# A convolution and scan kernel on one core: image pair 0 scans 131 steps ahead of pair 1

## The chip, the core and the metric

The kernel runs on one core of a Trainium2 chip. The core has a matrix engine (TensorE, PE in the rows; its weight loads are shown as PEld), a vector engine (VectorE, DVE), an activation engine (ScalarE, ACT), a general engine (GpSimd, POOL) and a sequencer for transfers (SyncE, SP). Each takes its own instructions in order and waits on semaphores for the others. The metric is the time of one execution on the device in microseconds (us), lower is better. The medians are of 3 runs. The profile is of one more execution, with the hardware's records switched on.

## What is computed

Four images of 48 channels and 128 x 128 pixels go through four layers, each added to its input after a group norm over the whole image (16 groups). All of it is in float32.

```python
x = x + L0(gn(x))   # channel attention: 1x1 conv, 3x3 depthwise, q k^T over pixels, softmax, v, 1x1
x = x + L1(gn(x))   # four scans
x = x + L2(gn(x))   # four scans with other weights
x = x + L3(gn(x))   # per pixel MLP: W1, gelu twice, layer norm, 3x3 and 1x1 conv of 8 channels, gate, W2

def step(w, b):                       # one step of a scan
    def f(carry, inp):                # carry: one line of 128 pixels, 48 channels
        nxt = inp + conv1d(carry, w, b)   # 5 taps along the line
        return nxt, nxt
```

The four scans of a layer go down the rows, back up, along the columns, and back. Each has 127 steps, and each step needs the line that the step before it made. The four images are independent until the end; only the group norm ties the pixels of one image together, and it has to see all of them.

## The kernel before, in words

**Layout.** An image's pixels lie two to a partition group: the 112 used partitions hold the channels of even pixels (LO) and odd pixels (HI). Images are stored by pairs: pair 0 is images 0 and 1, pair 1 is images 2 and 3. A line of one pair is 128 elements in each partition, and a scan step works on one pair.

**The attention (to 970.6 us).** For each image PE makes queries, keys and their gram product (`query_keys`, L834 to L849, 32 "pairs" of products per image, "qk" below) and then the output convolution (`output_conv`, L888, 16 groups of six products, "cv"). ACT stages the normalised input for both (`stage`, L625). The softmax of an image runs on DVE, ACT and PE in slots between the products of the next image. The order is qk0, qk1, cv0, qk2, cv1, qk3, cv2, cv3.

**The scans.** For layer and scan, for each of the 127 steps, both pairs take one step (both take part in one turn of the loop, here called a **beat**). A step of a pair is this chain: six matrix instructions on PE (three float32 products, each recorded twice: L927, L928, L930) add into a PSUM bank that already holds input plus bias; ACT copies the bank over the line in `image` (L718), and this copy releases the pair's next step. DVE has put input plus bias into the other bank of the pair meanwhile (`preload`, L1213, line 1213). In the second and fourth scan DVE also exchanges odd and even pixels of the finished lines for the next direction (`swap_part`, L1223, three copies of 256 elements for both pairs together, in three of every four slots). Lines are contiguous in scans one and two and strided in three and four.

**Between the layers (1676.5 to 1781.4 us).** The input of the layer comes back from DRAM in chunks of 2048 elements (`bring`, L399), DVE adds two of each four (L1233) and GpSimd the other two (L530), DVE takes the statistics (L1051), the sum is saved (L404), and ACT (L699) and DVE (L1254) normalise. PE waits.

**After the scans (2472.6 to 2648.3 us).** DVE (three of four parts) and GpSimd (one) add the residual and write 16 chunks in natural order (`natural`, recorded at L323, which both engines call), the chunks go to DRAM (L750) and come back as tokens, pixel major (L440). DVE takes statistics of all four images and `affine` (L1325) normalises image 0. Then the MLP runs image by image to the end.

**GpSimd elsewhere.** Early in the first scan it clears buffers (L498) and builds the banded weights of the 3x3 convolution with 120 small instructions (L510, L513, L517).

What sets the order is the program text: there is no planner. Each engine's list is written so that both pairs are in the same scan at the same step.

## Time and profile before

| | us |
|---|---|
| median of 3 runs (lowest to highest) | 2888.86 (2888.66 to 2891.61) |
| the profiled execution, its own time | 2902.14 |
| its span, first to last instruction | 2900.0 |
| PE busy | 2491.4 (86%) |
| DVE busy | 1597.3 (55%) |
| ACT busy | 1087.6 (38%) |
| POOL busy | 271.9 (9%) |
| mean granted clock of PE | 0.937 of 2.4 GHz |

The span in 40 slices (72.5 us each) shows PE at nine tenths or more nearly all the way, with a hole between the two scan layers and another behind the second. A busy PE is not a PE at its peak: the ends of matrix instructions are modelled. The granted clock is a share of 2.4 GHz and has two levels here, 1.0 and 0.5. The scan stretches hold 1016 beats in 1382 us, so a beat is the unit of what follows.

### The profile page before, as it was taken

To read this page: it belongs to the slowest core of one execution; us is meant where nothing else is said; L and a number is where in the kernel's file an instruction comes from. 1 tells how busy PE (TensorE), PEld (TensorE's weight loads), DVE (VectorE), ACT (ScalarE), POOL (GpSimd) and SP (SyncE) were. 2 spreads that over 40 slices of the span, in tenths; PEclk is the share of its full clock that TensorE was granted. 3 is DMA by queue.
4 is the path that set the end of the run, shared out by engine and by line. 5 is a ranking of instruction groups with operands and counts; after the bars stand their busy time and mean duration, and the time that the engine had idled before them with its cause. 6 is when DMAs were issued, how large, how long until landed. Compare 5 with 4: busy or idle time off the path is not lost.

```text
span 2900.0 us, 47470 instructions
## 1 busy us (share of the span) xinstructions
PE 2491.4 (86%) x18076; PEld 2178.8 (75%) x18076; DVE 1597.3 (55%) x3797; ACT 1087.6 (38%) x2617; POOL 271.9 (9%) x288
## 2 busy tenths in 40 slices
PE   1999999999999899999999914999999999104986
PEld 1999949949943599999999914999999999002443
DVE  2323223223322455885568875558855688775655
ACT  3533343343357344444444413444444444001221
POOL 1000000000000360000000041000000000335420
PEclk9999999999999999999999956999999999556998
DMA  8840000003001400000000076000000000474423
GB/s 147 143 78 2 1 1 1 1 0 88 1 0 44 88 1 1 2 2 1 1 2 1 2 201 147 1 1 2 2 1 1 1 1 2 130 235 170 117 87 87
DMA packets 51672, 130.17 MB, mean 45 GB/s; under 512 B 9120, under 2 KB 34048, under 8 KB 44896
## 3 DMA queue, kind: packets, MB, share of 16 engines
q1 hardware_dynamic: 48352, 113.92, 16.4%
q10 hardware_dynamic: 2976, 13.34, 1.5%
q8 instruction: 138, 2.26, 0.3%
q14 instruction: 78, 0.64, 0.1%
q0 software_dynamic: 128, 0.01, 0.0%
HBM read 76.91 MB, written 50.33 MB: 44 GB/s over the span
## 4 chain that ended last, share of the span: by engine, by line
PE 84%; DMA 6%; DVE 6%; issue 2%; ACT 1%; POOL 1%; SPq 0%; DVEq 0%; ACTq 0%; POOLq 0%
PE bank L927 17%; PE bank L928 15%; PE bank L930 15%; PE bank L834 13%; PE bank L888 11%; PE bank L849 3%; PE bank L839 3%; DMA flat_rows<-work 2%; DVE work L323 2%; DMA work<-saved 2%; PE bank L972 2%; PE bank L1030 1%; DMA work<-in_x 1%; DMA saved<-image 1%; PE bank L963 1%
## 5 line engine op out<-in xcount | busy, mean ns | idle before, releaser
L1213 DVE TENSOR_SCALAR bank<-image,scan_bias 112x128 f32<-112x128 f32 x2032 | 711.7, 360 | 354.8 <-ACT image L718 333.1
L718 ACT COPY image<-bank 112x128 f32<-112x128 f32 x2032 | 588.4, 290 | 795.1 <-PE bank L930 764.5
L927 PE MATMUL bank<-image,scan_wt 112*112 112x128 f32 x4064 | 816.9, 282 | 31.6 <-ACT image L699 16.8
L928 PE MATMUL bank<-image,scan_wt 112*112 112x126 f32 x4064 | 771.3, 271 | 0.0
L930 PE MATMUL bank<-image,scan_wt 112*112 112x126 f32 x4064 | 769.6, 270 | 0.0
L927 PEld LDWEIGHTS bank<-image,scan_wt 112*112 112x112 f32 x4064 | 557.2, 175 | 41.9 <-ACT image L699 27.2
L928 PEld LDWEIGHTS bank<-image,scan_wt 112*112 112x112 f32 x4064 | 581.8, 176 | 0.0
L930 PEld LDWEIGHTS bank<-image,scan_wt 112*112 112x112 f32 x4064 | 578.8, 176 | 0.0
L625 ACT ACTIVATE work<-image,gn_shift,gn_scale 48x567 f32<-48x567 f32 (+5 forms) x384 | 332.5, 898 | 348.9 <-PE bank L839 219.4
L834 PE MATMUL bank<-work 112*128 112x192 f32 x2304 | 424.4, 333 | 10.0 <-issue 10.0
L834 PEld LDWEIGHTS bank<-work 112*128 112x128 f32 x2304 | 375.8, 193 | 11.7 <-issue 11.2
L888 PE MATMUL bank<-work 112*112 112x512 f32 x768 | 333.0, 595 | 3.0 <-DVE work L1141 3.0
L888 PEld LDWEIGHTS bank<-work 112*112 112x112 f32 x768 | 135.8, 178 | 194.0 <-issue 190.8
L1109 DVE COPY work<-bank 128x384 f32<-128x384 f32 x128 | 71.4, 558 | 360.4 <-PE bank L839 276.6
L1051 DVE BATCH_NORM_STATS2 stats<-image 112x6 f32<-112x512 f32 (+2 forms) x240 | 152.9, 683 | 61.1 <-ACT image L597 45.1
L1162 DVE TENSOR_TENSOR image<-image,bank 112x512 f32<-112x512 f32 (+1 forms) x64 | 44.1, 690 | 238.3 <-PE bank L888 147.0
L809 PE MATMUL bank<-mean_var,group_flat 128*128 128x4 f32 x2 | 0.6, 366 | 169.7 <-DVE mean_var L1058 169.7
L323 POOL TENSOR_TENSOR work<-image,work 48x1024 f32<-48x1024 f32 x16 | 56.2, 3513 | 788.8 <-DVE image L1223 715.4
L809 PEld LDWEIGHTS bank<-mean_var,group_flat 128*128 128x128 f32 x2 | 0.5, 313 | 169.8 <-DVE mean_var L1058 169.8
L809 PE MATMUL bank<-mean_var,group_half 112*112 112x2 f32 (+2 forms) x12 | 2.5, 276 | 137.2 <-DVE mean_var L1058 137.2
L323 DVE TENSOR_TENSOR work<-image,work 48x1024 f32<-48x1024 f32 x48 | 98.6, 2053 | 35.4 <-DMA flat_rows<-work 33.4
L1223 DVE COPY work<-image 48x256 f32<-48x256 f32 x256 | 80.9, 316 | 66.5 <-ACT image L718 58.5
(137 smaller groups left out, 1639.0 us busy)
## 6 DMA issues: line engine op xcount, KB each, us to landing
work<-saved SPq DMA_DIRECT2D x64, 384.0 KB, 8.8
saved<-image SPq DMA_DIRECT2D x10, 1536.0 KB, 21.6
flat_rows<-work ACTq DMA_DIRECT2D x32, 384.0 KB, 7.3
image<-flat_rows SPq DMA_DIRECT2D x4, 3072.0 KB, 13.9
out<-image SPq DMA_DIRECT2D x8, 1536.0 KB, 8.1
saved<-image SPq DMA_DIRECT2D x12, 768.0 KB, 9.9
band<-in_x SPq DMA_DIRECT2D x16, 384.0 KB, 6.0
work<-in_x SPq DMA_DIRECT2D x16, 384.0 KB, 6.2
```

The costliest lines, as they stand in the source:

```text
L323: return eng.tensor_tensor(o[:, :, :, :, half], i0.rearrange("p g s k j -> p (g s) k j"), i1, ALU.add)
L625: last = nc.scalar.activation(dst.rearrange("p (k j) -> p k j", j=J2)[:, :, d[0]:d[1]], src, ACT.Identity, bias=gn_shift[part, b:b + 1], s ...
L718: nc.scalar.copy(line(g, along_w, at), state_bank(g, done)).then_inc(s_state[g], 1)
L834: last = mm(dst, (blk_z, blk_n)[buf][n % 2][:, o:o + 2 * J2], qk_w[buf][:, dy].rearrange("p a b -> p (a b)"), start=(t == 0), stop=(packed ...
L839: last = mm(dst[:, side * QK:(side + 1) * QK], blk_2[n % 2][:, side, sub, o:o + 2 * J2], qk_w2[:, side, :], start=False, stop=(side == 1))
L849: last = mm(bank_gram[0:QK, 0:QK], v, v, start=(i == 0 and c == 0), stop=(i == PAIRS - 1 and c == 3))
L888: last = mm(bank_out[sub][0:P, :], out_w[buf][:, dy, :], (blk_z, blk_n)[buf][n % 2][:, o:o + BLK * J2], start=(t == 0), stop=(t == len(pro ...
L927: mm(dst, wt[:, 1], src, start=False, stop=False, skip_group_check=True)
L928: mm(dst[:, 1:J2, :], wt[:, 0], src[:, 0:J2 - 1, :], start=False, stop=False, skip_group_check=True)
L930: mm(dst[:, 0:J2 - 1, :], wt[:, 2], src[:, 1:J2, :], start=False, stop=True, skip_group_check=True).then_inc(s_prod[g], 1)
L1051: return v.bn_stats(stat6[0:parts, b, ds(c * 6, 6)], src)
L1213: v.tensor_scalar(state_bank(g, done), line(g, along_w, src), scan_bias[:, 3 * layer + kind:3 * layer + kind + 1], None, ALU.add).then_inc ...
```

## The change

The change lets pair 0 run 131 steps ahead of pair 1 (`LEAD`). One function, `moment`, says for a pair and a beat in which layer, scan and step it is; 1204 beats (`BEATS`) take the place of 1016.

- **Beats 0 to 118** hold steps of pair 0 alone, one after each half of a qk3 pair (64), 7 around the softmax of image 3, and one after every second product of cv3 (48). cv2 therefore moves ahead of qk3. Pair 0 uses PSUM banks 5 and 6, pair 1 banks 2 and 3.
- **Beats 119 to 130** are pair 0 alone, with the group norm of pair 1 (`arrive`).
- **From beat 131** both pairs step in most beats. Each pair has two idle beats between its second and third scan, and a pause of 53 (`GAP`) between the layers. In that pause DVE adds two chunks in pieces of 512 elements and takes 32 statistics, one instruction per beat (`turn`), GpSimd adds the other six chunks in pieces of 512 and normalises half of the lines, and DVE and ACT normalise the rest. While one pair pauses, the other steps alone (beats 510 to 562 and 641 to 693).
- **Beats 1073 to 1203**: pair 1 alone. Pair 0 is converted: DVE does `natural` in 64 pieces of 256 elements, one per beat, GpSimd does two of four parts in pieces of 512, tokens are loaded, and 24 statistics and a norm follow.
- **Behind the last beat** the eight chunks of pair 1 are converted as before, by DVE (three parts) and GpSimd (one). `affine(0)` waits for the last conversion alone. The statistics of pair 1 (24) lie inside the MLP of image 0, its norm and `affine(2)` behind it.
- The exchange copies are per pair, 128 elements each, twice as many; in the fourth scan of the second layer there are none.
- GpSimd normalises all of pair 0 before its first scan and half of pair 1 (`normalise`); the buffers' clearing and the banded weights come after that. Loops of the MLP are unrolled. Buffers move; `xn` and several tiles of the MLP now lie in `work`.

The core of the diff ("..." marks what is left out):

```diff
+V_CHUNKS = (0, PER)
+P_CHUNKS = tuple(c for c in range(2 * PER) if c not in V_CHUNKS)
 PARTS = 4
-K_SPLIT = K2 // 4
+KQ = K2 // PARTS
+NBUF = 6
+PIECE = 512
+LAYER = PASSES * STEPS
+TURN_ROWS = 2
+ARRIVE = 11
+GAP = 2 + 10 * 4 + ARRIVE
+LEAD = 131
+SPAN = LAYER + TURN_ROWS
+END = 2 * SPAN + GAP
+BEATS = LEAD + END
+OUT_STATS = 90
+OUT_NORM = 114
+QK_BEATS = 64
+ORDER = (("qk", 0), ("qk", 1), ("cv", 0), ("qk", 2), ("cv", 1), ("cv", 2), ("qk", 3), ("cv", 3))
+QK_AT = tuple(NBLK * ORDER.index(("qk", b)) for b in range(NB))
+CV_AT = tuple(NBLK * ORDER.index(("cv", b)) for b in range(NB))
 TOK = 48
...
+        back = [cut(i * CHUNK, [CHUNK], P) for i in range(NBUF)]
+        nat = back[PER:NBUF]
+        swap_tmp = [cut(NBUF * CHUNK + g * 2 * J2, [J2, 2], P) for g in range(2)]
...
+        def moment(g, beat):
+            r = beat - g * LEAD
+            layer = int(r >= SPAN + GAP)
+            r -= layer * (SPAN + GAP)
+            if r >= 2 * STEPS + TURN_ROWS:
+                scan = min(PASSES - 1, (r - TURN_ROWS) // STEPS)
+                return layer, scan, r - TURN_ROWS - scan * STEPS
+            scan = 1 if r >= STEPS else 0
+            return layer, scan, r - scan * STEPS
...
+            return bank[(5, 2)[g] + done % 2][0:P, 0:2 * J2].rearrange("p (j q) -> p j q", q=2)
...
+            def normalise(layer, g, kq):
+                pool.wait_ge(s_gn, (3 + g) if layer == 0 else (5 + g))
+                for s in range(2):
+                    saved_once(pool, g, layer, s, kq)
+                    for q in range(2):
+                        for h in range(2):
+                            cols = part_of(g, q, s, kq, slice(h, h + 1), 2)
+                            b = 2 * g + q
+                            last = nc.gpsimd.tensor_scalar(cols, cols, gn_scale[0:P, b:b + 1], gn_shift[0:P, b:b + 1],
+                                                           ALU.mult, ALU.add)
+                last.then_inc(s_norm[g], 1)
+            for kq in range(PARTS):
+                normalise(0, 0, kq)
+                if kq == 0:
+                    pool.wait_ge(s_norm[0], 1)
+                    pool.sem_inc(s_state[0], 1)
+            for kq in range(2, PARTS):
+                normalise(0, 1, kq)
+            pool.wait_ge(s_x1, TWO + NB * 2 * NBLK)
+            pool.wait_ge(s_norm[1], 2)
...
+                for c in P_CHUNKS:
+                    loaded(pool, g, c)
+                    for u in range(CHUNK // PIECE):
+                        o = g * 2 * IMG + c * CHUNK + u * PIECE
+                        dst = image[0:P, o:o + PIECE]
+                        last = nc.gpsimd.tensor_tensor(dst, dst, back[c % NBUF][:, u * PIECE:(u + 1) * PIECE], ALU.add)
+                    last.then_inc(s_kept_p, 1)
+                for kq in range(2, PARTS):
+                    normalise(1, g, kq)
...
+            def natural_part(e, sides):
+                loaded_end(pool, e)
+                if e >= 2:
+                    pool.wait_ge(s_flat[e % 2], 32 * (e // 2))
+                for i, a in enumerate(sides):
+                    for k0 in range(0, BLK, BLK // 2):
+                        last = natural(nc.gpsimd, e, a, 1, k0, k0 + BLK // 2)
+                    last.then_inc(s_res_p, 1)
+                    pool.wait_ge(s_res_p, pool_done(e) + i + 1 - len(sides))
+            pool.wait_ge(s_norm[1], 4)
+            pool.wait_ge(s_state[0], 2 * (LAYER + 1))
+            for e in range(2 * PER):
+                natural_part(e, (0, 1))
+            pool.wait_ge(s_res, 2 * PER)
...
+            def take_step(g, beat):
+                layer, scan, n = moment(g, beat)
+                if n >= STEPS:
+                done = scan * STEPS + n
+                if n < STEPS - 1:
+                    act.wait_ge(s_pre[g], layer * LAYER + done + 2)
+                act.wait_ge(s_prod[g], layer * LAYER + done + 1)
+                nc.scalar.copy(line(g, along_w, at), state_bank(g, done)).then_inc(s_state[g], 1)
...
+            stage(6, 0)
+            beat = 0
+            for n in range(NBLK):
+                for j in range(8):
+                    take_step(0, beat)
+                    beat += 1
+                    if j < 6:
+                        stage_piece(6 + (n + 1) // NBLK, (n + 1) % NBLK, j)
+            for j in range(7):
+                take_step(0, beat)
+                beat += 1
+                if j == 0:
...
+            query_keys(QK_AT[3], 3 * PAIRS, {}, lambda: None, 2 * 2 * NBLK, next_step)
+            for i in range(7):
+                next_step()
+                if i == 1:
+                    key_norms(3)
+                elif i == 3:
+                    mixing(3)
+                elif i == 4:
+                    tap_weights(3)
+            output_conv(3, CV_AT[3], {}, bank[0:4], next_step)
...
+            def turn(g, tau):
+                part, u = divmod(tau - 2, 4)
+                if part in (0, 4):
+                    c = V_CHUNKS[part // 4]
+                    if u == 0:
+                        loaded(dve, g, c)
+                    o = g * 2 * IMG + c * CHUNK + u * PIECE
+                    dst = image[0:P, o:o + PIECE]
+                    v.tensor_tensor(dst, dst, back[c % NBUF][:, u * PIECE:(u + 1) * PIECE], ALU.add)\
+                        .then_inc(s_kept_v, 1)
+                else:
+                    c = part - 1 - (part > 4)
+                    s, m = c // PER, c % PER
+                    q, k = u // 2, 2 * m + u % 2
+                    if u == 0:
+                        kept(dve, g, c)
+                    src = img(slice(0, P), 2 * g + q, s, slice(k * BLK, (k + 1) * BLK), slice(0, J2))
+                    last = take_stats(P, 2 * g + q, s * NBLK + k, src.rearrange("p k j -> p (k j)"))
+                    if part == 9 and u == 3:
+                        last.then_inc(s_stat, 1)
+            def arrive(g, layer, left):
+                r = 3 if layer == 0 else 4 + g
+                c0, c1 = 2 * g, 2 * g + 2
...
+            def natural_ops(e, tau):
+                a, k0 = tau // 4, tau % 4 * 2
+                if tau == 0:
+                    loaded_end(dve, e)
+                    if e >= 2:
+                        dve.wait_ge(s_flat[e % 2], 32 * (e // 2))
+                last = natural(v, e, a, 0, k0, k0 + 2)
+                if tau == 7:
+                    last.then_inc(s_res, 1)
...
+            def exchange(g, beat, late):
+                layer, scan, n = moment(g, beat)
+                if scan == 1 or (scan == 3 and layer == 0):
+                    lag = 5 if scan == 1 else 3
+                    m = 2 * (n - lag) + (late if g == 0 else late - 1)
+                    if n < STEPS and m >= 0 and m % 4 < 3:
+                        swap_part(g, scan == 3, K2 - 1 - m // 4 - (scan == 1), m % 4)
+                    elif n == STEPS and late == g:
                         for i in ((K2 - 1,) if scan == 1 else ()) + (1,):
                             for m in range(3):
...
+            def full_beat(beat):
+                on = [g * LEAD <= beat < g * LEAD + END for g in range(2)]
+                for g in range(2):
+                    if on[g]:
+                        slot(g, beat)
+                    for e in range(2):
+                        if on[e]:
+                            exchange(e, beat, g)
+                    if on[g]:
+                        preload(g, beat)
+                if LEAD - ARRIVE <= beat < LEAD:
+                    arrive(1, 0, LEAD - beat)
+                for g in range(2):
+                    layer, scan, n = moment(g, beat) if beat >= g * LEAD else (1, 0, 0)
+                    tau = n - STEPS
+                    if tau < 0 or scan < PASSES - 1:
+                        continue
+                    if layer == 0 and 2 <= tau < GAP - ARRIVE:
+                        turn(g, tau)
+                    elif layer == 0 and tau >= GAP - ARRIVE:
+                        arrive(g, 1, GAP - tau)
+                    elif layer == 1 and g == 0:
+                        leave(tau)
...
```

## Rows read from the trace of the kernel before

**Rows 1.** Windows by stage: length, busy us (count) per engine, granted clock, DMA, GB/s.
```profile
0.00:970.60 970.60, 901.02 (x4963) 702.96 (x4964) 296.16 (x607) 405.06 (x477) 13.69 (x20) 0.99 0.21 39
970.60:985.70 15.10, 2.23 (x15) 1.59 (x13) 11.58 (x24) 7.84 (x7) 1.59 (x1) 0.71 0.47 104
985.70:1676.50 690.80, 688.52 (x6096) 683.32 (x6096) 471.12 (x1395) 293.98 (x1015) 70.36 (x124) 0.99 0.03 6
1676.50:1781.40 104.90, 2.14 (x8) 1.81 (x9) 72.82 (x100) 22.86 (x9) 41.76 (x8) 0.52 0.82 219
...
2472.60:2648.30 175.70, 1.18 (x4) 1.00 (x4) 134.35 (x111) 0.20 (x1) 78.86 (x88) 0.51 0.59 197
2648.30:2900.00 251.70, 207.66 (x896) 104.86 (x896) 139.80 (x168) 63.46 (x92) 65.62 (x48) 0.90 0.35 100
```

**Rows 2.** Timeline of one beat of the second scan: start, length, engine, line.
```profile
1200.85 0.27 PEld L927 LDWEIGHTS bank<-image,scan_wt 112*112 112x112 f32 x2
...
1201.37 0.38 PE L930 MATMUL bank<-image,scan_wt 112*112 112x126 f32 x2
...
1201.84 0.27 ACT L718 COPY image<-bank 112x128 f32<-112x128 f32 x1 [0.38 <-PE bank L930]
...
1202.16 0.27 PEld L927 LDWEIGHTS bank<-image,scan_wt 112*112 112x112 f32 x2
```

**Rows 3.** Windows of scans two, three and four, L718 on ACT alone.
```profile
1156.00:1321.00 165.00, 67.03 (x252) 1.00 0.01 2
1325.00:1498.00 173.00, 75.82 (x253) 0.99 0.01 1
1499.00:1675.00 176.00, 81.42 (x251) 1.00 0.01 1
```

**Rows 4.** Timeline of the first scan's first beat, at the lower clock.
```profile
985.66 0.45 PEld L927 LDWEIGHTS bank<-image,scan_wt 112*112 112x112 f32 x2 [10.38 <-ACT image L699]
...
987.36 0.27 ACT L718 COPY image<-bank 112x128 f32<-112x128 f32 x1 [2.37 <-PE bank L930]
```

**Rows 5.** Windows of that start, and of 50 us with GpSimd at work.
```profile
985.00:990.90 5.90, 5.21 (x25) 5.24 (x26) 2.18 (x7) 0.80 (x3) 5.90 (x4) 0.51 0.00 0
1000.00:1050.00 50.00, 50.00 (x459) 50.00 (x458) 26.99 (x77) 20.25 (x76) 44.26 (x82) 1.00 0.19 34
```

**Rows 6.** Windows of the last stage, PE alone: granted clock behind the busy time.
```profile
2709.00:2712.00 3.00, 2.44 (x14) 1.00 0.00 0
...
2738.00:2742.00 4.00, 2.18 (x11) 0.97 1.15 348
2742.00:2748.00 6.00, 6.00 (x13) 0.50 0.21 62
```

**Rows 7.** L323 on DVE: duration ns min/median/max.
```profile
L323 DVE TENSOR_TENSOR work<-image,work x48: 1217/1221/3858, 2475.0 to 2606.4; 48x1024 f32<-48x1024 f32 x48
```

**Rows 8.** L323 on POOL, in the same columns.
```profile
L323 POOL TENSOR_TENSOR work<-image,work x16: 2786/3843/3868, 2474.5 to 2600.2; 48x1024 f32<-48x1024 f32 x16
```

**Rows 9.** Timeline of L1347 in image 0, GpSimd idle.
```profile
2688.01 0.23 DVE L1347 TENSOR_SCALAR work<-work 128x128 f32<-128x128 f32 x1
```

**Rows 10.** The same line in image 1, L575 running on GpSimd.
```profile
2742.57 0.69 DVE L1347 TENSOR_SCALAR work<-work 128x128 f32<-128x128 f32 x1
```

**Rows 11.** The page's costliest groups: busy, mean ns, idle before and its releaser.
```profile
L1213 DVE TENSOR_SCALAR bank<-image,scan_bias 112x128 f32<-112x128 f32 x2032 | 711.7, 360 | 354.8 <-ACT image L718 333.1
...
L1051 DVE BATCH_NORM_STATS2 stats<-image 112x6 f32<-112x512 f32 (+2 forms) x240 | 152.9, 683 | 61.1 <-ACT image L597 45.1
...
L1223 DVE COPY work<-image 48x256 f32<-48x256 f32 x256 | 80.9, 316 | 66.5 <-ACT image L718 58.5
```

**Rows 12.** Groups by line, with the page's columns.
```profile
L510 POOL TENSOR_SCALAR band_tmp<-identp,gates 128x128 f32<-128x128 f32 x48 | 29.0, 605 | 4.6
...
L1325 DVE TENSOR_SCALAR image<-image,gn_scale,gn_shift 128x6144 f32<-128x6144 f32 (+1 forms) x4 | 13.9, 3470 | 0.0
...
L1371 DVE TENSOR_TENSOR work<-bank,gates 128x512 f32<-128x512 f32 x8 | 5.2, 687 | 38.5 <-PE bank L1011 38.5
```

More of the change, by code:

```diff
@@ L857, in query_keys @@
                         gram_pair(i - 1)
+                    if i < PAIRS and beats is not None:
+                        beats()
                     if i in slots:
@@ L1204, in _, with add_blocks @@
-            for n in range(NBLK):
-                last = add_block(NB - 1, n, (2 * NB - 1) * NBLK + n + 2 if n < NBLK - 1 else None)
-            last.then_inc(s_stat, 1)
-            def preload(layer, done, scan, n, g):
+            def add_blocks(b, then, between=None):
+                for n in range(NBLK):
+                    end = n == NBLK - 1
+                    last = add_block(b, n, None if end else CV_AT[b] + n + 2, between if end else None)
+                    if end:
+                        last.then_inc(s_stat, 1)
+                    then(n)
@@ L1387, in mlp @@
                     take_tokens(b + 1, g)
[L1388 removed]
+                if even_more and b:
                     affine(b + 2)
```

835 lines of the change are left out of this document (435 added, 400 removed).

## The prediction, as put on record

> **What bounds the kernel now.** I first read the windows by stage [rows 1]. PE works through all of the attention but for starts and short waits. In the scans its records have no holes, and between the layers (104.9 us) and behind the second layer (175.7 us) it does nearly nothing, at half the clock. These two holes and the 15.1 us ahead of the first scan, 296 us in all, are what a lead of one pair can fill.
>
> Next the timeline of one beat [rows 2]. Weights are asked for at 1200.85, the last matrix instruction ends at 1201.37 + 0.38 = 1201.75, ACT copies from 1201.84 to 1202.11, the next weights start at 1202.16. That is 1.31 us, one chain of one pair, with 0.05 and 0.09 us between its links and nowhere a wait for the other pair. PE is as full: twelve instructions in the same 1.31 us, 0.655 us for each pair. So both limits lie on each other: a beat costs the same 1.31 with two pairs as it would with one. Counting the copies gives 165 / 126 = 1.31 us a beat in scan two, 173 / 126.5 = 1.37 in scan three (strided lines) and 176 / 125.5 = 1.40 in scan four, with its exchange [rows 3].
>
> This is the price of the change: a beat with one pair alone saves nothing, and there are 1204 beats for 1016.
>
> **The change, part by part, if nothing else interferes.** I add up the span and compare it with 2900.0.
>
> - *Attention with 112 steps in it.* PE is the limit there, so each step costs its 0.655 us: 970.6 + 112 x 0.655 = 1044. The seven steps around the softmax, which was hidden before, stand alone: 7 x 1.32 = 9, up to 20 with the softmax's hand-overs; I take 13. End of cv3: 1057. ACT and DVE are under half busy there [rows 1], which covers the copies and preloads; without this cover a step would cost up to its whole chain, 112 x 0.66 = 74 us more.
> - *Beats with both pairs, 832.* 246 at 1.31 (the leader in scan two), 254 at 1.37 (leader in scan three), 205 at 1.40 (one pair in scan four of the first layer) and 127 at 1.37 (scan four of the second layer, whose exchange is gone): 322 + 348 + 287 + 174 = 1131.
> - *Beats with one pair, 253.* 69 on contiguous lines at 1.32 = 91; 184 on strided lines at 1.36 = 250. In beats 510 to 562 DVE has preload 0.36, one statistic or addition of 0.69, and 1.5 copies, which I estimate at 0.23 [rows 9, 11]: with hand-overs 1.49, so 36 beats pay 0.13 more, 5 us. Scans end at 1057 + 1131 + 346 = 2534, 61 us later than the 2472.6 of before.
> - *Behind the scans.* The conversion of 16 chunks took 2475.0 to 2607.6, 132.6 us [rows 7]; half is 66. With 2.4 us ahead and 3.5 for `affine` [rows 12] the MLP starts at 2606, where before it started at 2648.3.
> - *MLP.* It took 251.7 us [rows 1]. Added are 24 statistics x 0.683 = 16.4 [rows 11], of which the wait of L1371, 38.5 / 4 = 9.6 us per image [rows 12], hides a part: 7. The norm and `affine(2)`, 3.5 us plus about 4.5 for the norm's round trips, now stand between images 0 and 1: 8. Bounds: 0 and 30. Together 267.
>
> Sum: 2606 + 267 = **2873**, 27 us (0.9%) faster. The 296 us that are filled have shrunk to this because 188 beats were added (about 255 us) less 119 hidden in the attention.
>
> **What is added to it: the clock.** PE's granted clock was 1.0 in the scans and fell to 0.5, that is from 2.4 to 1.2 GHz, in every hole [rows 1]. At the low level a pair's chain is 987.36 - 985.66 = 1.70 to the copy, + 0.27 + 0.05 = 2.02 us [rows 4], 2.06 on strided lines. Before, with two pairs, the low clock lasted only briefly: from 985.7 PE had no pause, and it was back at full clock by 990.9 [rows 5, 1]. A lone beat leaves PE idle in each beat, at the low level too (0.4 of 2.0), so nothing like this unbroken work is there to raise it.
>
> What no row shows is a long stretch of short pauses. The nearest: PE was busy 2.44 of 3.0 us and kept its clock; it was busy 2.18 of 4.0 us and lost it [rows 6]. A smooth lone beat (0.82 of 1.32, from 1200.94 to 1201.75) lies between. A lone beat stretched to 1.78 us (next part) has 0.82 of 1.78, nearer to the row that lost. I take the fall in the last stretch (131 beats x 0.70 = 92) and in beats 510 to 562 (53 x 2.06 = 109 for 77, +32), half of it in 641 to 693 (53 x 0.70 = 37, so 19) and 4 us in beats 119 to 130. Sum: 147. Bounds: nothing, and 170.
>
> The Trainium skill ("TensorE: Matmul & The Clock Gate", "A second HAM failure mode: psum-queue depth-cycling") describes a kernel whose short pauses between groups of products, while it cycled PSUM banks, made the clock swing between its levels. By that the clock falls in lone beats; no run here shows yet whether it stays down.
>
> **What is added to it: DVE and GpSimd in each other's way.** A DVE addition of 1024 elements from two SBUF tiles took 1.22 us and up to 3.86 with GpSimd's addition beside it [rows 7]; GpSimd's took 2.79 to 3.87 [rows 8]. The difference is the other's duration: one waits for the whole of the other. A small single-source DVE instruction took 0.23 and, with GpSimd working, 0.69 [rows 9, 10]. Preloads are spared: with GpSimd busy 44 of 50 us there were 38 beats in 50 us as elsewhere [rows 5].
>
> - *Last stretch.* GpSimd's pieces of 512 are half of 2.79, 1.39 us; a DVE piece of 256 is about 0.4. Alternating they take 1.78, more than the chain's 1.36, while the 32 pieces last. It is this that pulls PE apart; at the low clock 1.78 fits below 2.06 and costs nothing itself. If the clock holds: 32 x 0.42 = 13 us.
> - *Exchange copies.* These lie ahead of the preloads in DVE's list, so the whole beat waits with them. No row has one beside GpSimd; I go by rows 9 and 10. GpSimd's normalising instructions of 512 elements are longer than the 0.6 us of the 128-element one [rows 12], I estimate 1.6. Behind beat 131 come 8 to 16 of those, six clearings and 120 small ones; each exchange copy waits for one, 0.3 to 1.6 us. I estimate 15 + 7 + 11 = 33 us there, 8 us behind each pause of a pair, and 3 in beats 510 to 562. I take 37 of these 52; bounds 0 and 70.
>
> The Trainium skill ("SBUF — State Buffer", "SBUF: two separate sides") calls this port pair an exclusive lock, held for a whole instruction, taken by GpSimd and by DVE when it reads two SBUF inputs or copies in a two-port mode. By it the exchange copies are caught as the additions are, which speaks against this change; rows 7 to 10 agree with it, for additions at 3.86 against 1.22.
>
> **Sum.** 2873 + 147 + 37 = 3057 of span. The profiled execution's own time was 2902.14 and the median of the runs 2888.86, so I scale by 2888.86 / 2900.0: **3045 us**, 5.4% slower.
>
> **Rivals.**
>
> 1. *It all fits.* The clock holds in lone beats and the lock costs little: 2873 to 2890 of span, 2862 to 2880 measured, faster. For it: the smooth lone beat has pauses of 0.5 us only, and the first of rows 6 kept its clock with about as much in total [rows 6]. Against: rows 7 and 8 are the very instructions of the last stretch. It decides at whether PE's pause in a lone beat stays near 0.5 us. Chance 0.12.
> 2. *The clock holds, the lock costs.* 2873 + 13 + 52 + about 15 in the pauses = 2953, measured 2942, slower. Chance 0.14.
> 3. *Only the last stretch goes cold* and the copies are not caught: 2873 + 92 = 2965, measured 2954. I count it with the forecast's range.
> 4. *The lead is not there*: the steps inside the attention wait for ACT (its staging instructions lie in the same list as the copies) or for GpSimd's normalising, each step costs its chain: 74 more on top of the forecast, 3120. Chance 0.06.
>
> The forecast, with the third, has 0.68. The range is 2890 to 3110: it leaves out the first rival and most of the fourth. About 0.2% is what a measurement of this kernel can tell from no change. Faster by more: 0.13; within: 0.03; slower: 0.84.
>
> **What would show it.** The granted clock of the windows of the lone stretches: 0.5 and 2.0 us between copies if I am right, 1.0 and 1.32 to 1.36 if the first rival is. PE without holes until cv3's end near 1057, pair 1's first step some 18 us behind it. Exchange copies (L1223's successor) with a mean well over 0.23 us while GpSimd works, and `natural` pieces near 1.8. The MLP at 267 us. The prediction is wrong if the clock holds through single-pair beats, or if the rate in two-pair beats is not that of before.

## The result, and the profile after

The kernel after takes 3007.62 us (median of 4 runs, 2998.74 to 3012.81) against 2890.24 us before (2888.66 to 2894.28): a ratio of 1.0401, 95% interval 1.0373 to 1.0429. It is 4.0% slower, inside the predicted range and 37 us below the predicted 3045.

The profiled execution has a span of 2996.9 us, against 2900.0. From its page, busy time by engine and two rows of the 40 slices (75 us each):

```profile
PE 2689.8 (90%) x18080; PEld 2308.4 (77%) x18080; DVE 1608.3 (54%) x4237; ACT 1013.2 (34%) x2620; POOL 389.0 (13%) x442
...
PE   2989999999999989999998898899999987764896
PEclk9999999999998989999997596699999975556998
```

The clock row of before, for comparison:

```profile
PEclk9999999999999999999999956999999999556998
```

PE is busy 198 us more than before for the same work. The clock rows say why: before, the low digits were in the hole between the layers, in the one behind the scans and in the MLP, and now they lie where PE works. The windows by stage, in the columns of [rows 1] (length, then busy us and count of PE, PEld, DVE, ACT and POOL, then clock, DMA share, GB/s):

```profile
0.00:1070.40 1070.40, 987.30 (x5688) 784.40 (x5688) 336.56 (x731) 419.12 (x591) 38.83 (x52) 0.99 0.19 36
1070.40:1095.50 25.10, 18.51 (x92) 15.96 (x92) 13.14 (x31) 9.54 (x22) 16.96 (x18) 0.66 0.26 59
1095.50:1602.00 506.50, 501.13 (x4512) 499.07 (x4512) 390.42 (x1326) 203.03 (x753) 75.31 (x126) 1.00 0.05 11
1602.00:1712.30 110.30, 82.85 (x331) 67.90 (x332) 82.47 (x182) 19.33 (x61) 45.56 (x40) 0.54 0.42 115
1712.30:1815.00 102.70, 102.59 (x930) 102.39 (x928) 79.96 (x272) 41.72 (x156) 0.00 (x0) 1.00 0.01 2
1815.00:1922.50 107.50, 84.10 (x330) 68.72 (x331) 54.69 (x115) 19.07 (x61) 45.81 (x40) 0.53 0.44 103
1922.50:2424.40 501.90, 499.28 (x4518) 498.08 (x4517) 340.14 (x1133) 202.56 (x753) 1.61 (x2) 1.00 0.01 2
2424.40:2685.40 261.00, 205.72 (x784) 165.97 (x784) 103.26 (x226) 35.27 (x132) 71.09 (x103) 0.51 0.27 73
2685.40:2737.90 52.50, 0.00 (x0) 0.00 (x0) 51.84 (x25) 0.03 (x1) 34.77 (x16) 0.50 0.69 177
2737.90:2996.90 259.00, 208.29 (x900) 105.96 (x900) 155.83 (x200) 63.56 (x93) 59.03 (x48) 0.90 0.40 123
```

They are, in order: attention to the end of cv3; beats 119 to 130; both pairs (beats 131 to 509); pair 1 alone while pair 0 pauses (510 to 562); both; pair 0 alone (641 to 693); both (694 to 1072); pair 1 alone (1073 to 1203); conversion of pair 1; MLP. Wherever both pairs step the clock is 1.00, and in each of the three long stretches of lone beats (beats in which one pair steps alone) it is 0.51 to 0.54, that is 1.2 GHz nearly all the way.

One beat of the last stretch in the timeline (start, length, engine, line):

```profile
2600.90 0.27 ACT L782 COPY image<-bank 112x128 f32<-112x128 f32 x1 [1.75 <-PE bank L1033]
...
2601.22 0.77 PE L1030 MATMUL bank<-image,scan_wt 112*112 112x128 f32 x2 [0.41 <-ACT image L782]
2601.46 0.68 DVE L1186 BATCH_NORM_STATS2 stats<-image 128x6 f32<-128x512 f32 x1
...
2602.20 0.62 PE L1033 MATMUL bank<-image,scan_wt 112*112 112x126 f32 x2
2602.92 0.27 ACT L782 COPY image<-bank 112x128 f32<-112x128 f32 x1 [1.75 <-PE bank L1033]
```

From copy to copy it is 2.02 us. DVE's statistics end at 2602.14 and keep nothing waiting; PE idles 0.41 us while ACT copies, and then each of its instructions runs at the low clock. It is the chain of the cold first beat of before [rows 4], now in nearly all of the 237 beats of these stretches (median 2.02 us in each).

### The profile page after: what moved, and what is told of

It reads as the page before. It is cut to its first block, busy times and chain, and to the rows that moved or that the text cites. A ratio compares the mean times of both kernels' runs of the same rounds, so it can differ in the third digit from the quotient of the medians.

```text
span 2996.9 us, 47545 instructions
## 1 busy us (share of the span) xinstructions
PE 2689.8 (90%) x18080; PEld 2308.4 (77%) x18080; DVE 1608.3 (54%) x4237; ACT 1013.2 (34%) x2620; POOL 389.0 (13%) x442
## 4 chain that ended last, share of the span: by engine, by line
PE 86%; DVE 7%; ACT 3%; issue 2%; DMA 1%; ACTq 0%; POOL 0%; SPq 0%; DVEq 0%; POOLq 0%
PE bank L1030 19%; PE bank L1033 16%; PE bank L1031 16%; PE bank L923 13%; PE bank L982 11%; PE bank L941 3%; PE bank L928 3%; ACT image L782 2%; DVE work L382 2%; PE bank L1163 2%; PE bank L1105 1%; DMA work<-in_x 1%; DVE stats L1186 1%; PE bank L1096 1%; DVE image L1393 1%
## 5 line engine op out<-in xcount | busy, mean ns | idle before, releaser
L1030 PE MATMUL bank<-image,scan_wt 112*112 112x128 f32 x4064 | 885.4, 301 | 125.4 <-ACT image L782 124.8
L1031 PE MATMUL bank<-image,scan_wt 112*112 112x126 f32 x4064 | 826.4, 287 | 0.0
L1033 PE MATMUL bank<-image,scan_wt 112*112 112x126 f32 x4064 | 826.2, 286 | 0.0
L1030 PEld LDWEIGHTS bank<-image,scan_wt 112*112 112x112 f32 x4064 | 602.5, 188 | 227.6 <-ACT image L782 199.0
L1031 PEld LDWEIGHTS bank<-image,scan_wt 112*112 112x112 f32 x4064 | 634.6, 190 | 0.0
L1033 PEld LDWEIGHTS bank<-image,scan_wt 112*112 112x112 f32 x4064 | 631.7, 191 | 0.0
L728 ACT ACTIVATE work<-image,gn_shift,gn_scale 48x567 f32<-48x567 f32 (+3 forms) x384 | 335.8, 899 | 263.9 <-PE bank L928 146.8
L565 POOL TENSOR_SCALAR image<-image,gn_scale,gn_shift 112x512 f32<-112x512 f32 x80 | 69.5, 908 | 1157.2 <-DVE gn_shift L1207 1157.0
L1186 DVE BATCH_NORM_STATS2 stats<-image 112x6 f32<-112x512 f32 (+1 forms) x240 | 160.0, 686 | 45.2 <-ACT image L691 42.0
L382 POOL TENSOR_TENSOR work<-image,work 48x512 f32<-48x512 f32 x48 | 84.8, 1787 | 684.4 <-issue 618.4
L1393 DVE COPY work<-image 48x128 f32<-48x128 f32 x384 | 95.3, 248 | 114.4 <-ACT image L782 113.6
L612 POOL TENSOR_TENSOR image<-image,work 112x512 f32<-112x512 f32 x48 | 62.5, 1342 | 528.3 <-DVE image L1393 528.3
L1393 DVE COPY image<-image 48x128 f32<-48x128 f32 x384 | 94.4, 246 | 59.7 <-ACT image L782 53.1
```

What stands on the lines that cost most here:

```text
L382: return eng.tensor_tensor(o[:, :, k0:k1, :, half], i0, i1, ALU.add)
L728: last = nc.scalar.activation(dst.rearrange("p (k j) -> p k j", j=J2)[:, :, d[0]:d[1]], src, ACT.Identity, bias=gn_shift[part, b:b + 1], s ...
L1030: mm(dst, wt[:, 1], src, start=False, stop=False, skip_group_check=True)
L1031: mm(dst[:, 1:J2, :], wt[:, 0], src[:, 0:J2 - 1, :], start=False, stop=False, skip_group_check=True)
L1033: mm(dst[:, 0:J2 - 1, :], wt[:, 2], src[:, 1:J2, :], start=False, stop=True, skip_group_check=True).then_inc(s_prod[g], 1)
L1186: return v.bn_stats(stat6[0:parts, b, ds(c * 6, 6)], src)
```

## The experiments

All ratios are against the kernel before, which ran beside each of them. The first four ask whether the clock makes lone beats slow, the next four what DVE and GpSimd cost each other, the last three where terms of my sum came from that the clock doesn't explain.

### Give PE as much work in a lone beat as in a full one

```diff
+            FILL_AT = ((LEAD - ARRIVE, BEATS),)
+            FILL = 3
+            def filler(beat):
+                live = [g for g in range(2) if g * LEAD <= beat < g * LEAD + END and moment(g, beat)[2] < STEPS]
+                if len(live) != 1 or not any(lo <= beat < hi for lo, hi in FILL_AT):
+                    return
+                dst = bank[4][0:P, 0:2 * J2]
+                for i in range(FILL):
+                    mm(dst, scan_wt[:, 0, i], identp[0:P, 0:2 * J2], start=True, stop=True)
...
                         step(g, beat)
+                filler(beat)
```

> The kernel after, with three more 112x128 products (two matrix instructions each, as in a step) issued by PE behind the step of every beat that has one pair only, into a PSUM bank that nobody reads. PE then has twelve matrix instructions in every beat, as in a two-pair beat. Clock theory: the four stretches of lone beats return to 1.0 of the clock; beats 1073 to 1203 take 1.32 to 1.36 us instead of 2.01 (260.8 us become 175 to 190), beats 510 to 563 70 to 79 instead of 110.3, 641 to 694 70 to 72 instead of 107.5, 119 to 131 16 instead of 25.1; in all 150 to 170 us less, about 2850 us, which is also below the 2889 of the kernel before. Rival, lone beats are slow because DVE and GpSimd hold each other up or because the chain of one pair is that long: beats stay at 2.0 us or get longer by the added products, 3010 to 3100 us. Middle case: the clock returns but 32 beats beside GpSimd's conversion pieces take 1.78 us, 13 us of the gain lost.

Measured: 2875.04 us, ratio 0.9934 (0.9910 to 0.9958). More work on the busiest engine takes 135 us off (0.0467 of 2890, the difference of the two ratios; the spans differ by 133.6), less than the 150 to 170 expected, and the kernel with the lead is now faster than before. The three stretches of lone beats:

```profile
1597.70:1693.10 95.40, 82.14 (x650) 75.94 (x649) 83.53 (x182) 19.52 (x61) 45.97 (x40) 0.96 0.46 133
1795.80:1870.20 74.40, 72.36 (x649) 71.03 (x648) 56.13 (x114) 19.28 (x62) 44.63 (x36) 1.00 0.60 150
2372.30:2550.90 178.60, 176.67 (x1565) 174.76 (x1565) 108.65 (x226) 35.41 (x132) 72.63 (x103) 0.99 0.39 107
```

The clock is up and the last stretch went from 261.0 to 178.6 us, the second from 107.5 to 74.4. The first kept 95.4 where 70 to 79 was expected; DVE is busy 83.5 of them, which is taken up below. These 16 to 25 us are most of what is missing.

```diff
-            FILL_AT = ((LEAD - ARRIVE, BEATS),)
+            FILL_AT = ((END, BEATS),)
```

> The same three added products, but only in beats 1073 to 1203, the last stretch. Clock theory: this stretch alone gains 70 to 86 us and ends near 2930; the granted clock of 510 to 563 and 641 to 694 stays at 0.5 and their beats at 2.03 to 2.08 us. Rival: no gain or a loss, 3005 us or more.

Measured: 2924.23 us, ratio 1.0101 (1.0071 to 1.0131). The last stretch has 180.3 us, the other two keep 110.4 and 107.5 at clocks of 0.54 and 0.53. The gain goes where the products go, and nowhere else.

```diff
-            FILL = 3
+            FILL = 1
```

> One added product of 128 columns instead of three, in all lone beats: at full clock PE is busy about 1.04 of 1.32 us instead of 0.82. If the clock needs PE to have no pause at all, it still falls: about 3000 us. If a shorter pause of about 0.28 us is enough, the time is that of the three products, near 2850. I expect something between, with the clock changing back and forth in the stretches: 2850 to 2960. Rival, the clock is not the cause: no change, 3005 to 3030.

Measured: 2875.32 us, ratio 0.9944 (0.9918 to 0.9970). One product does as much as three: the last stretch has clock 1.00 and 177.1 us. My middle case, a clock that changes back and forth, was wrong there. It came true in beats 510 to 562, where the same product left the clock at 0.80 on average (it was 0.95 in beats 641 to 693):

```profile
1602.50:1698.60 96.10, 75.27 (x436) 63.26 (x436) 83.78 (x182) 19.40 (x61) 45.45 (x40) 0.80 0.47 132
...
2378.80:2555.90 177.10, 146.62 (x1045) 120.68 (x1044) 110.09 (x226) 35.01 (x132) 72.18 (x103) 1.00 0.40 108
```

In beats 510 to 562 it stood at 0.50 from 1620 to 1630 us, where the beats took 2.3 to 2.6 us with DVE and GpSimd in each other's way, and at 1.00 from 1640 to 1670, where they took 1.3 to 1.8.

> One added product of 32 columns in every lone beat, a quarter of the one product of 128 that did as much as three. PE's pause of about 0.5 us shrinks by some 0.05 to 0.1. If what matters is that the pause is interrupted or slightly shorter, the clock stays up as with one product of 128: near 2875. If it is the busy time in the beat, it falls as without: near 3005. I expect the latter, with at most the stretch 641 to 694 up: 2970 to 3010.

```diff
-            FILL = 3
+            FILL = 1
...
-                    mm(dst, scan_wt[:, 0, i], identp[0:P, 0:2 * J2], start=True, stop=True)
+                    mm(dst[:, 0:32], scan_wt[:, 0, i], identp[0:P, 0:32], start=True, stop=True)
```

Measured: 3000.86 us, ratio 1.0372 (1.0346 to 1.0399), with 0.53 and 0.54 for the clock in all three stretches and 258.9 us in the last:

```profile
2429.00:2687.90 258.90, 232.58 (x1045) 215.71 (x1044) 102.25 (x226) 34.93 (x132) 71.25 (x103) 0.53 0.27 74
```

In all these kernels the added product starts right behind the step's last one, so it makes PE's work longer and its one pause shorter. PE's first product of a beat of the last stretch, with the pause ahead of it in brackets, while the clock is up; first in the kernel after, then with 32 columns, then with 128:

```profile
2426.05 0.47 PE L1030 MATMUL bank<-image,scan_wt 112*112 112x128 f32 x2 [0.41 <-ACT image L782]
2429.30 0.47 PE L1030 MATMUL bank<-image,scan_wt 112*112 112x128 f32 x2 [0.29 <-ACT image L782]
2500.37 0.48 PE L1030 MATMUL bank<-image,scan_wt 112*112 112x128 f32 x2 [0.19 <-ACT image L782]
```

The first two fell to the low clock a few beats later and stayed there, the third kept 1.00. A product in the beat is not enough by itself. Whether the longer work or the shorter pause held the clock these runs can't tell, for they changed together.

### DVE and GpSimd

> The kernel of the three added products, in which GpSimd clears its six buffers six times instead of once, behind beat 131: 30 more clearings of 2048 elements, about 1.87 us each, 56 us, while DVE does exchange copies in both of every three beats' slots and PE is full with both pairs. My prediction's theory, an exchange copy waits for the whole of the GpSimd instruction that runs: each beat in these 56 us is held up by 0.5 to 1.9 us, beats 131 to 254 take 25 to 40 us more than the 168.0 of the first of these runs. Rival, exchange copies share with GpSimd: 0 to 3 us more. The small instructions of GpSimd (0.46 and 0.61 us), which the profile after shows beside copies of 0.22 to 0.31 us, speak for the rival; the six copies that met a clearing there, all above 0.45 us, for the theory.

```diff
+            for i in range(5):
+                for m in range(NBUF):
+                    nc.gpsimd.memset(back[m][32:HALF, :], 0.0).then_inc(s_clear, 1)
+                pool.wait_ge(s_clear, NBUF * (i + 1))
             for m in range(NBUF):
                 nc.gpsimd.memset(back[m][32:HALF, :], 0.0).then_inc(s_back_gap, 1)
```

Measured: 2901.99 us, ratio 1.0025 (1.0012 to 1.0039), 0.9% above the same kernel without the added clearings. Between the copies of beats 131 and 254 lie 196.2 us instead of 168.0: 28.2 us for 30 clearings. DVE's timeline there, and GpSimd's beside it:

```profile
1099.28 1.60 DVE L1410 COPY image<-image 48x128 f32<-48x128 f32 x1
1100.91 0.35 DVE L1397 TENSOR_SCALAR bank<-image,scan_bias 112x128 f32<-112x128 f32 x1
1101.30 1.41 DVE L1410 COPY image<-work 48x128 f32<-48x128 f32 x1
...
1097.18 9.10 POOL L581 MEMSET work<- 32x2048 f32 x5
```

A copy of 0.23 us takes 1.0 to 1.6 us when it meets a clearing, and each of the 30 copies in these 55 us does. The preloads (into PSUM) keep their 0.35 us but for ten of 39, and those are recorded as starting while the copy ahead of them still waits. The theory holds for long instructions. In the kernel after the copies met few of them. By line, minimum, median and maximum in ns:

```profile
L1393 DVE COPY image<-image x384: 222/224/1635, 1093.4 to 2258.1; 48x128 f32<-48x128 f32 x192
L565 POOL TENSOR_SCALAR image<-image,gn_scale,gn_shift x80: 789/816/1380, 711.5 to 1917.9; 112x512 f32<-112x512 f32 x80
L591 POOL TENSOR_SCALAR band_tmp<-identp,gates x48: 599/606/650, 1104.9 to 1177.5; 128x128 f32<-128x128 f32 x48
```

Counted over all 1152 copies of the kernel after, those above 0.45 us are 25: seven beside GpSimd's normalising instructions, six beside the clearings, nine beside its additions, three beside the 120 small instructions that build the banded weights; 83 more ran beside these small ones and took less than 0.45 us. I had counted on each of them to hold a copy for 0.3 us.

> The kernel of the three added products, in which ACT instead of DVE does the exchange copies of pair 1 in beats 514 to 562, while DVE has the additions and statistics of pair 0's pause. In the first of these runs these beats took 1.80 us although the clock was up (95.4 us for 53). Theory, DVE's list is the limit there (42.2 us busy of 45): some 70 copies of 0.25 us and their hand-overs leave it, the stretch takes 72 to 80 us, the kernel 15 to 22 us less than with the three products alone, about 2857. Rival, the additions of GpSimd hold DVE's up and these set the beat: 88 to 95 us, no more than 5 us gained.

```diff
+                if beat in ACT_SWAPS:                                  # ACT's list, ahead of the step's copy
+                    act.wait_ge(s_state[1], 3 * STEPS + moment(1, beat)[2])
+                    act_exchange(beat)
...
+                if g == 1 and beat in ACT_SWAPS:                       # DVE's list
+                    swaps[1] += len(late_parts(beat, late))
+                    return
```

Measured: 2857.53 us, ratio 0.9874 (0.9842 to 0.9906). This beats both kernels: 1.3% below before, 5% below after. The stretch has 85.9 us instead of 95.4, with 61.1 us of DVE instead of 83.5, and most of its beats now take 1.33 us (median, where it was 1.66):

```profile
1601.20:1687.10 85.90, 77.07 (x650) 74.90 (x649) 61.11 (x113) 40.74 (x130) 44.27 (x39) 0.94 0.52 148
```

So DVE's list, with its waits for GpSimd, was the limit of these beats once the clock was up. This is its timeline in the first of these kernels, the one with three products and DVE's exchange:

```profile
1641.78 0.35 DVE L1392 TENSOR_SCALAR bank<-image,scan_bias 112x128 f32<-112x128 f32 x1
1642.16 0.69 DVE L1198 BATCH_NORM_STATS2 stats<-image 112x6 f32<-112x512 f32 x1
1642.87 0.23 DVE L1405 COPY image<-image 48x128 f32<-48x128 f32 x1
1643.20 0.24 DVE L1405 COPY image<-work 48x128 f32<-48x128 f32 x1
1643.47 0.35 DVE L1392 TENSOR_SCALAR bank<-image,scan_bias 112x128 f32<-112x128 f32 x1
...
1644.78 0.34 DVE L1392 TENSOR_SCALAR bank<-image,scan_bias 112x128 f32<-112x128 f32 x1
```

From preload to preload it is 1.69 us with two copies and 1.31 with one, and DVE has no pause worth the name; GpSimd is idle here. The expected 72 to 80 was missed for one reason, a single addition of DVE:

```profile
1623.99 8.30 DVE L1460 TENSOR_TENSOR image<-image,work 112x512 f32<-112x512 f32 x1
1632.22 0.34 DVE L1415 TENSOR_SCALAR bank<-image,scan_bias 112x128 f32<-112x128 f32 x1
...
1619.44 12.30 POOL L619 TENSOR_TENSOR image<-image,work 112x512 f32<-112x512 f32 x10
```

Ten GpSimd additions follow each other without a gap from 1619.44 to 1631.74, and DVE's, put at 1623.99, ends only behind the last of them. It waited for a row of instructions, not for one. Meanwhile the preload behind it is late and pair 1 stands still: this one beat takes 7.85 us, and the clock is down for the next three (2.0 to 2.6 us).

```diff
+                            cols = cols[:, :, w] if layer == 0 else cols[:, 0:1, w]    # w: one element
...
-                        dst = image[0:P, o:o + PIECE]
+                        dst = image[0:P, o:o + 1]
...
+                    if e < 2 * PER:                                    # pair 0's chunks
+                        last = nc.gpsimd.memset(spare_word, 0.0)
+                        last.then_inc(s_res_p, 1)
...
+                        continue
```

> The kernel of the three added products with GpSimd's additions and normalising of the pauses one element wide and its conversion of pair 0 in the last stretch replaced by a clearing of one element; this part of the computation is left out. If DVE and GpSimd in each other's way cost what I predicted for a full clock (13 us in the last stretch, 8 behind each pause, 15 in the pauses): 40 to 50 us less than with the three products. From the profiles after I now expect less: 6 us in the last stretch (178.6 to 173), 8 to 12 in beats 510 to 563, 2 to 3 in 641 to 694, in all 15 to 22 us, about 2856.

Measured: 2853.87 us, ratio 0.9864 (0.9838 to 0.9889), 0.7% or 20 us below the three products alone. The stretches have 82.4, 72.9 and 174.7 us instead of 95.4, 74.4 and 178.6. This kernel leaves out GpSimd's part of the additions and the normalising in the pauses, and of pair 0's conversion. So all of GpSimd's long work in the pauses and the last stretch costs some 18 us at full clock, 13 of them in beats 510 to 562:

```profile
1600.80:1683.20 82.40, 77.88 (x649) 73.87 (x648) 69.42 (x182) 19.61 (x62) 10.78 (x35) 0.98 0.55 154
```

DVE's list is whole in this kernel, and many of the beats still alternate between 1.32 and about 1.7 us. What is gone are the beats of 2.3 to 2.65 us that the kernel with three products has while GpSimd adds, in which exchange copies took 1.1 to 1.3 us. The 95.4 us of these beats come from both, the length of DVE's list and its waits for GpSimd. The second reading, made from the profile after, was right, and the first, my prediction's 40 to 50, was not.

> The kernel with ACT's exchange copies and three added products in the lone beats, and three added products also in beats 64 to 70, the seven steps around the softmax of image 3, which took 18 to 20 us at half the clock in all profiles so far. Theory, the clock explains a part: with the clock up the stretch takes 12 to 15 us, beats 71 to 76 no longer start cold, 3 to 6 us less than without, near 2853. Rival, the softmax's hand-overs between DVE, ACT and PE set it and the added products lie in their way: the same 18 us or a few more, 2857 to 2862.

```diff
-            FILL_AT = ((LEAD - ARRIVE, BEATS),)
+            FILL_AT = ((QK_BEATS, QK_BEATS + 7), (LEAD - ARRIVE, BEATS))
...
             for i in range(7):
                 next_step()
+                filler(beat - 1)
```

Measured: 2859.51 us, ratio 0.9876 (0.9851 to 0.9901), the same as without. The stretch itself went from 18.2 to 15.3 us, with the clock at 1.00 where it was 0.72 (in the kernel after 19.6 us at 0.57). In the profiled execution this is not to be seen in the whole time, because a DVE addition waited 8.31 us for GpSimd in beats 510 to 562, as before, and another 9.66 us in beats 641 to 693.

### Two terms that the clock does not explain

Both pairs together ran faster in the kernel after than before. ACT's copies (length, busy and count, clock) in beats 255 to 380, 385 to 505 and 957 to 1070:

```profile
1262.00:1428.00 166.00, 67.11 (x250) 1.00 0.01 2
1434.00:1595.00 161.00, 65.57 (x239) 1.00 0.01 2
2270.00:2420.00 150.00, 61.59 (x227) 1.00 0.01 2
```

That is 166 / 125 = 1.33, 1.35 and 1.32 us a beat, where before had 1.37 and 1.40 on strided lines [rows 3]. The copies have 0.27 us where before had 75.82 / 253 = 0.30. In a few places of the second and the last of these windows the old value returns; the first place of the last one:

```profile
2296.37 0.27 ACT L782 COPY image<-bank 112x128 f32<-112x128 f32 x1 [0.39 <-PE bank L1033]
2297.03 0.31 ACT L782 COPY image<-bank 112x128 f32<-112x128 f32 x1 [0.40 <-PE bank L1033]
...
2300.41 0.30 ACT L782 COPY image<-bank 112x128 f32<-112x128 f32 x1 [0.35 <-PE bank L1033]
...
2301.77 0.27 ACT L782 COPY image<-bank 112x128 f32<-112x128 f32 x1 [0.35 <-PE bank L1033]
```

Such places, four beats each, are 32 beats apart (beats 977, 1009 and 1041, and 414, 446 and 478), and in each the strided lines that the two pairs work on are 8 bytes apart modulo 256 bytes, which is as near as they come here. Before, with both pairs at the same step, the two offsets were always the same.

> The kernel before with one edit: pair 1's image lies 32 elements (128 bytes) further on in its buffer, so that the same line of the two pairs no longer lies at the same place modulo 256 bytes. In the profile after the strided two-pair beats took 1.325 us where before had 1.37, and of 127 beats with the pairs in scans four and three only twelve took 1.36, in three groups 32 beats apart, where the two lines' numbers differ by 65 to 61, 1 to -3 and -63 to -67. Theory, beats of 1.36 come from lines at the same place modulo 256 bytes: scan three goes from 1.37 to 1.33 a beat and scan four from 1.40 to about 1.34, in both layers together 20 to 27 us less, about 2866. Rival, the rate came from the copies being per pair or from the exchange of 128 instead of 256 elements: no change, 2889.

```diff
-        image = sb("image", [128, COLS])
+        image = sb("image", [128, COLS + 2 * PAD])                     # PAD = 32
...
-        image6 = image[0:P, :].rearrange("p (g s k j q) -> p g s k j q", g=2, s=2, k=K2, q=2)
+        image6 = image[0:P, :].rearrange("p (g n) -> p g n", g=2)[:, :, 0:2 * IMG].rearrange(
+            "p g (s k j q) -> p g s k j q", s=2, k=K2, q=2)
...
+        def at_of(t):
+            return t * IMG + t // 2 * PAD
```

Measured: 2862.95 us, ratio 0.9893 (0.9871 to 0.9915), 31 us less for 128 bytes of padding. Scans three and four of its first layer, to be read against [rows 3]:

```profile
1325.00:1494.00 169.00, 68.09 (x254) 0.99 0.01 1
1494.60:1662.00 167.40, 68.19 (x253) 1.00 0.01 2
```

They have 1.33 and 1.32 us a beat. The theory holds, and scan four's whole excess with its exchange was of this kind. It is a matter of strided lines alone: scans one and two, on contiguous lines, have a median of 1.31 us a beat with the padding and without it. The edit also unrolls GpSimd's loop between the layers, but that stage didn't get shorter, and the scans hold the gain.

> The kernel before with GpSimd's conversion pieces of 1024 elements cut into two of 512, as the kernel after has them. The conversion behind the last scan step took 66 us for eight chunks by my prediction, and 52.5 us in the profile after. Theory, DVE and GpSimd wait for each other's whole instruction, and a GpSimd piece of 2.8 to 3.8 us makes the longest of these waits: with halves the 132.6 us become about 105, the kernel about 25 us less. Rival, the shorter conversion came from how the chunks are brought and stored: no change in the 132.6 us, 2885 to 2895.

```diff
-                        natural(nc.gpsimd, bp, q, m, 1, 1).then_inc(s_res_p, 1)
+                        natural(nc.gpsimd, bp, q, m, 1, 1, 0, BLK // 2)
+                        natural(nc.gpsimd, bp, q, m, 1, 1, BLK // 2, BLK).then_inc(s_res_p, 1)
```

Measured: 2879.79 us, ratio 0.9960 (0.9943 to 0.9978). GpSimd's and DVE's pieces, against [rows 7, 8]:

```profile
L323 DVE TENSOR_TENSOR work<-image,work x48: 1217/2416/2536, 2464.9 to 2583.2; 48x1024 f32<-48x1024 f32 x48
L323 POOL TENSOR_TENSOR work<-image,work x32: 1483/2471/2562, 2464.5 to 2579.6; 48x512 f32<-48x512 f32 x32
```

The longest of DVE's waits is gone (2.54 instead of 3.86 us), and from the first piece to the end of the last it is now 120 us instead of 132.6. That is half of what I expected. For eight chunks it makes 60; that the kernel after needs 49 us (of its 52.5) has another part that no run took apart; how its chunks are brought and stored is my guess.

Both edits of this section together in the kernel before:

> The kernel before with both small edits, pair 1's image 32 elements further on and GpSimd's conversion pieces in halves; no lead. If their gains add (28 us from the scans, 12 from the conversion): 0.985 to 0.986 of before, 2850 to 2853 us, level with the best kernel with the lead (0.987). If they got in each other's way, 0.989 as with the first alone.

Measured: 2854.53 us, ratio 0.9876 (0.9860 to 0.9892): between the two expectations and level with the best kernel that has the lead. A few lines in the kernel before bring as much as the whole lead with its repairs. The kernels with the lead have both gains already, for their pairs work on different lines and GpSimd's pieces are halves; beyond these two, what the lead itself gains, repairs included, can't be told from nothing here (0.9874 against 0.9876).

## Why the prediction was right, step by step

**Beats with one pair save nothing.** Right, and it is the base of the result: 1204 beats for 1016. The count of them was four short, at no cost in the sum: behind beat 118 there are 828 beats with both pairs and 257 with one, not 832 and 253, because each pair has its two idle beats in both layers.

**The clock, 147 us.** Right in sign and near in size, with the parts less near than their sum: 135 us between the kernel after and its version with three products. Stretch by stretch, predicted and measured (after less with the products): last stretch 92 and 82; beats 510 to 562 32 and 15; beats 641 to 693 19 and 33; beats 119 to 130 4 and 5. For beats 641 to 693 the full fall was priced at 37. The half chance in 641 to 693 was a hedge that the profile didn't bear out: this stretch fell like the others. In 510 to 562 the step that failed is the 77 us at full clock: it takes 95.4 with GpSimd at work and 82.4 without, and the second rival had 15 for the pauses where 13 lie between these two. The clock itself fell in all of them and stayed down: the granted clock is 0.50 from 1610 to 1712 and from 2435 to 2685 us. The Trainium skill ("TensorE: Matmul & The Clock Gate", "A second HAM failure mode: psum-queue depth-cycling") tells of a kernel whose short pauses between groups of products made the clock swing between its two levels. The trace agrees that it falls in beats with short pauses; it didn't swing back here.

**DVE against GpSimd, 37 us.** The mechanism is right and the size was off. The excess over 1.313 us a beat behind beat 131 is 166.1 - 123 x 1.313 = 4.6 us and I had 33; behind the pauses it is 0 to 1 where I had 8 each; in beats 510 to 562 I had 3, and 110.3 - 53 x 2.02 is 3.2. What failed is the number of meetings. GpSimd's normalising instructions take 0.82 us and not the 1.6 that I estimated, and are over sooner; the 120 small ones, counted at 11 us, hold hardly a copy. The tell that I named, an exchange mean well over 0.23, failed: it was 0.25. By the Trainium skill ("SBUF — State Buffer", "SBUF: two separate sides") the pair of ports is held for a whole instruction; the clearings agree (1.6 us for a copy of 0.22); beside small instructions the trace shows next to nothing of it.

**Both pairs, 1131 us.** With four more idle beats of one pair (5 us) I had 1136 for 836 beats; the three windows have 506.5 + 102.7 + 501.9 = 1111, of which 5 are the copies' waits. The step that failed is taking 1.37 and 1.40 for a property of strided lines. They belonged to two pairs at the same line, and a lead undoes this: a gain of some 30 us that I had not seen.

**Attention, 1057.** Measured 1070.4. The 112 steps in it cost 1070.4 - 19.6 - 970.6 = 80 us and not 73, 0.72 us each. The softmax stretch took 19.6 and not 13, at a clock of 0.57 (3 to 4 us of it, by the run with filled beats 64 to 70: 15.3 against 18.2 and 19.6; the clock term had left this stretch out).

**Behind the scans.** Conversion and norm 52.5 us against 72; MLP 259.0 against 267.

**Sum.** From 3057: attention +13, beats 119 to 130 +5, both pairs with the copies' lock -59, 510 to 562 -2, 641 to 693 +18, last stretch -9, conversion -19, MLP -8. That makes 2996, and the span is 2996.9. The sum was 60 us of span too high because three gains, 30 us in the scans, 29 in the lock and 19 in the conversion, outweighed what came late. That only 37 us are left in the medians is luck in part: I scaled down by 12 us from a profiled execution slower than its median, and the profiled execution of the kernel after, with 2998.74 us, was the fastest of its four.

**The rivals.** "It all fits" would have been 2862 to 2880: it is the time of the version with filled beats, 2875. Its condition was not met. Its sum came out right with errors against each other: in that version both pairs took 23 us less than it had and the conversion 19 less, while beats 510 to 562 took 18 more and the attention 12 more. "The clock holds, the lock costs" at 2942 was wrong twice over: the clock fell, and all the lock's parts at full clock come to some 18 us in the pauses and the last stretch and to some 5 behind beat 131. "The lead is not there" is excluded by the attention's 80 us for 112 steps.

## What to carry to other kernels

Before you let one of two interleaved chains run ahead, ask what the matrix engine's clock does while it runs alone: here the second chain was also what kept 2.4 GHz, and one product that nobody reads, in each beat, was worth 4.6%. It gave back what the lead had cost and little more. When two streams march in step through one buffer, shift one by half of 256 bytes and measure; here it gave 1.1%, for strided lines. Work that is hidden beside a chain isn't free if it shares the queue of an engine in the chain: count that engine's list for one beat, and keep GpSimd's long runs away from DVE's additions.

## What the runs showed that I had not expected

- **Two pairs' lines at the same offset modulo 256 bytes cost 0.035 to 0.08 us a beat** of 1.32, in ACT's strided copy (0.27 to 0.30 us) and in the wait for it. The Trainium skill ("SBUF — State Buffer", "SBUF: two separate sides") has PE, ACT and DVE's own ports never waiting on anyone. Here 32 elements of padding changed ACT's copies from 75.82 / 253 = 0.300 to 68.09 / 254 = 0.268 us, on strided lines, and the kernel's time by 1.1%. The two don't agree, and the measurement decides. Which of the other engines the copies met isn't settled.
- **A DVE addition can be kept out by a whole row of GpSimd additions**, 8.30 us in one profile, 8.31 and 9.66 us in another, where the usual wait was 1.49 - 0.69 = 0.8 us. It appeared only in the two kernels where ACT did the exchange copies; why only there no run shows.
